# A GRU step on one core: the products of c ahead of those of r with one signal for both, and both vocabulary units of a block together, with one signal that also stands for the z products

## The reference

```python
x = emb_table[input_ids]                      # 2048 x 50 x 128
xp = einsum('bth,hk->btk', x, kernel) + b_i   # k = 3 * 128: z, r, h
def step(h, xt):
    rec = h @ rec_kernel + b_r
    xz, xr, xh = split(xt, 3);  rz, rr, rh = split(rec, 3)
    z = sigmoid(xz + rz)
    r = sigmoid(xr + rr)
    hh = tanh(xh + r * rh)
    h_new = z * h + (1 - z) * hh
logits = h_at_last_position @ emb_table.T     # 2048 x 12501, written out in float32
```

## Time and profile before

| | |
|---|---|
| median of 3 runs | 1207.63 us (1206.48 to 1207.8) |
| profiled execution: its own time | 1205.95 us |
| profiled execution: span from the first to the last instruction | 1204.1 us |
| TensorE busy, share of the span | 1064.9 us, 88% |
| VectorE busy | 798.4 us, 66% |
| ScalarE busy | 693.7 us, 58% |
| GpSimd busy | 763.7 us, 63% |
| mean granted TensorE clock, share of full speed | 0.989 |
| stage B, about | 91 to 591 us from the span's start |
| stage C, about | 591 to 974 us |
| stage D, about | 974 to 1124 us |
| tail, about | 1124 to 1204 us |

### The profile page before, as it was taken

How to read it: one execution, slowest core, us unless ns; L and a number is a source line. 1 busy time by engine, 2 the same in 40 slices (tenths; PEclk the granted TensorE clock), 3 DMA queues, 4 the chain that set the end, 5 groups by cost and what they waited for, 6 DMA issues and landing times.

```text
span 1204.1 us, 17546 instructions
## 1 busy us (share of the span) xinstructions
PE 1064.9 (88%) x6031; PEld 804.9 (67%) x6031; DVE 798.4 (66%) x1481; ACT 693.7 (58%) x1203; POOL 763.7 (63%) x812
## 2 busy tenths in 40 slices
PE   7968777877777778777899999999999999999997
PEld 6964444444444444444588888888888888888775
DVE  5745555555555555555677777888888887777644
ACT  4443444444444444444477777777777788888543
POOL 0017777777777777777777777777777777663000
PEclk9989999999999999999999999999999999999999
DMA  8986565656565656565588889989899999997799
GB/s 259 350 320 175 167 175 166 176 166 175 167 176 167 175 167 175 166 175 167 169 258 288 290 295 297 297 294 297 291 296 291 296 298 331 310 306 270 257 356 324
DMA packets 127495, 294.29 MB, mean 244 GB/s; under 512 B 18096, under 2 KB 33456, under 8 KB 127408
## 3 DMA queue, kind: packets, MB, share of 16 engines
q0 software_dynamic: 51200, 157.34, 45.3%
q1 hardware_dynamic: 76208, 135.84, 31.2%
HBM read 171.30 MB, written 121.81 MB: 243 GB/s over the span
## 4 chain that ended last, share of the span: by engine, by line
PE 56%; POOL 26%; issue 11%; DMA 5%; DVE 1%; ACT 0%; SPq 0%; DVEq 0%; ACTq 0%
POOL gathered L369 26%; PE x_ps L452 6%; PE x_ps L453 6%; PE x_ps L454 6%; PE r_ps L419 3%; DMA out_dram<-logits 3%; PE c_ps L419 3%; PE r_ps L432 3%; PE z_ps L432 3%; PE z_ps L419 3%; PE r_ps L433 2%; PE r_ps L436 2%; PE c_ps L432 2%; PE c_ps L433 2%; PE c_ps L436 2%
## 5 line engine op out<-in xcount | busy, mean ns | idle before, releaser
L369 POOL DMA_INDIRECT gathered<-gate_table,index x800 | 761.8, 952 | 338.1 <-issue 229.4
L570 ACT ACTIVATE table_rows<-r_ps,zr_bias 128x512 f32<-128x512 f32 (+1 forms) x250 | 151.2, 605 | 200.7 <-PE r_ps L427 162.6
L704 DVE SCALAR_TENSOR_TENSOR c_ps<-c_ps,bias_sb,table_rows 128x512 f32<-128x512 f32 (+1 forms) x250 | 162.8, 651 | 132.1 <-PE c_ps L427 98.6
L572 ACT ACTIVATE z_ps<-z_ps,zr_bias 128x512 f32<-128x512 f32 (+1 forms) x250 | 144.2, 577 | 182.4 <-PE z_ps L427 143.0
L562 ACT ACTIVATE logits<-x_ps,nan_row 128x512 f32<-128x512 f32 (+1 forms) x325 | 214.4, 678 | 42.8 <-PE x_ps L454 27.9
L709 DVE TENSOR_TENSOR table_rows<-z_ps,state 128x512 f32<-128x512 f32 (+1 forms) x250 | 145.0, 580 | 113.6 <-ACT z_ps L572 113.4
L419 PE MATMUL r_ps<-ident,gathered 128*128 128x128 f32 x800 | 107.6, 248 | 119.3 <-issue 107.6
L713 DVE SCALAR_TENSOR_TENSOR c_ps<-z_ps,table_rows 128x512 f32<-128x512 f32 (+1 forms) x250 | 147.7, 591 | 59.8 <-ACT table_rows L579 59.4
L419 PEld LDWEIGHTS r_ps<-ident,gathered 128*128 128x128 f32 x800 | 84.9, 141 | 138.2 <-issue 131.5
L716 DVE TENSOR_TENSOR state<-table_rows,c_ps 128x512 f32<-128x512 f32 (+1 forms) x250 | 145.3, 581 | 26.1
L579 ACT ACTIVATE table_rows<-c_ps,bias_sb 128x512 f32<-128x512 f32 (+1 forms) x250 | 149.7, 599 | 16.2 <-PE c_ps L419 14.7
(11 more groups left out here) (97 smaller groups left out, 1538.8 us busy)
## 6 DMA issues: line engine op xcount, KB each, us to landing
out_dram<-logits SPq DMA_DIRECT2D x192, 512.0 KB, 4.5
gate_table<-table_rows SPq DMA_DIRECT2D x24, 768.0 KB, 5.5
gathered<-gate_table,index POOLq DMA_INDIRECT x800
emb_rows<-in_L_rec_emb_table_dram SPq DMA_DIRECT2D x48, 256.0 KB, 5.8
out_dram<-logits SPq DMA_DIRECT2D x8, 213.0 KB, 3.7
logits<-in_r_input_ids_dram SPq DMA_DIRECT2D x1, 400.0 KB, 4.8
logits<-in_r_input_mask_dram SPq DMA_DIRECT2D x1, 400.0 KB, 6.2
gate_table<-table_rows SPq DMA_DIRECT2D x2, 192.0 KB, 9.3
```

The lines of the kernel that those rows point to most:

```text
L369: nc.gpsimd.indirect_dma_start(tile_rows(slot, n).bitcast(F32), None, table, bass.IndirectOffsetOnAxis(ap=index[:, tile, b.t:b.t + 1], axi ...
L570: nc.scalar.activation(r, r_bank, ACT.Sigmoid, bias=zr_bias[:, 1:2]).then_inc(s_r, 1)
L704: nc.vector.scalar_tensor_tensor(out=c_bank, in0=c_bank, scalar=bias_sb[:, 1, 2:3], in1=r, op0=ALU.add, op1=ALU.mult).then_inc(s_scaled, 1)
```

## The change

It does four things.

1. In `step`, the products of c are issued ahead of those of r, and only the last product of r raises `s_rec`, once for a block. Sigmoid r and the scaling on VectorE both wait for that one signal.
2. In a wide block both units stand ahead of the c rows, as they already do in a narrow block. The new `units` of `schedule` gives each block how many units stand in front of the c rows (2 in stages C and D, 0 in B) and behind them (always 0).
3. A unit's first bank no longer has its own signal: `s_unit` is raised once for a pair, with the last product of unit 1. Both copies wait for it, in the tail too.
4. In a block with units `s_z_in` is not raised. Sigmoid z waits for `s_unit` of the block's pair, which is raised later on the same engine than the z products. In stage B sigmoid z waits for `s_z_in` as before.

The place of the copies on ScalarE stays: ahead of tanh in a narrow block (`early`), behind it in a wide one.

```diff
 def schedule(T):
-    return order, 2 * T, lambda g: g >= 2 * T, [range(0, 4), range(4, 6), range(6, 8)]
+    def units(g):
+        if g < 2 * T:
+            return 0, 0, False
+        return (2, 0, False) if order[g][2] == LANE else (2, 0, True)
+
+    return order, 2 * T, units, [range(0, 4), range(4, 6), range(6, 8)]
...
 def unit(pair, j, bank):
-                nc.tensor.matmul(bank[:, 0:even], low, embT_hi[:, bass.ds(pair.v0, even)],
-                                 start=False, stop=True).then_inc(s_unit, 1)
+                last = nc.tensor.matmul(bank[:, 0:even], low, embT_hi[:, bass.ds(pair.v0, even)],
+                                        start=False, stop=True)
+                if j == UPP - 1:
+                    last.then_inc(s_unit, 1)
...
                 if not b.split:
+                    add_state(c_bank, h, 2, True)
                     add_state(r_bank, h, 1, False).then_inc(s_rec, 1)
-                    add_state(c_bank, h, 2, True).then_inc(s_rec, 1)
                     add_rows(z_bank, b, 0, True)
-                    add_state(z_bank, h, 0, False).then_inc(s_z_in, 1)
+                    z_done = add_state(z_bank, h, 0, False)
                 else:
                     pe.wait_ge(s_state_hi, blocks[b.prev].parts)
+                    add_high(c_bank, high, 2, True)
                     add_high(r_bank, high, 1, False)
-                    add_high(c_bank, high, 2, True)
                     pe.wait_ge(s_state_lo, blocks[b.prev].parts)
+                    add_low(c_bank, low, 2)
                     add_low(r_bank, low, 1).then_inc(s_rec, 1)
-                    add_low(c_bank, low, 2).then_inc(s_rec, 1)
                     add_rows(z_bank, b, 0, True)
                     add_high(z_bank, high, 0, False)
-                    add_low(z_bank, low, 0).then_inc(s_z_in, 1)
+                    z_done = add_low(z_bank, low, 0)
+                if not b.front:
+                    z_done.then_inc(s_z_in, 1)
                 if b.vocab >= 0:
                     vocabulary(b.vocab)
-                if b.pair >= 0:
-                    unit_beside(b.pair, 0)
-                    if b.width < LANE:
-                        unit_beside(b.pair, 1)
+                for w in b.front:
+                    unit_beside(w)
                 pe.wait_ge(s_scaled, g + 1)
                 add_rows(c_bank, b, 2, False).then_inc(s_turned, 1)
-                if b.pair >= 0 and b.width == LANE:
-                    unit_beside(b.pair, 1)
+                for w in b.behind:
+                    unit_beside(w)
...
 def copy_unit(u, j, bank):
-                act.wait_ge(s_unit, UPP * u + j + 1)
+                act.wait_ge(s_unit, u + 1)
...
 def gate(g, b):
-                act.wait_ge(s_rec, 2 * g + 1)
+                act.wait_ge(s_rec, g + 1)
                 nc.scalar.activation(r, r_bank, ACT.Sigmoid, bias=zr_bias[:, 1:2]).then_inc(s_r, 1)
-                act.wait_ge(s_z_in, g + 1)
+                if b.front:
+                    act.wait_ge(s_unit, b.front[-1] // UPP + 1)
+                else:
+                    act.wait_ge(s_z_in, b.alone)
                 nc.scalar.activation(z_bank, z_bank, ACT.Sigmoid, bias=zr_bias[:, 0:1]).then_inc(s_z, 1)
...
 def update(g, b):
-                dve.wait_ge(s_rec, 2 * g + 2)
+                dve.wait_ge(s_rec, g + 1)
```

More of the change, by code:

```diff
@@ L39 @@
     vocab: int = -1
-    pair: int = -1
+    front: range = range(0)
+    behind: range = range(0)
+    early: bool = False
+    alone: int = 0
 @dataclass
@@ L57, in schedule @@
     order = [lanes[0], lanes[1]] * T + [lanes[2], a, lanes[2], b] * (T // 2) + [a, b] * (T - T // 2)
-    return order, 2 * T, lambda g: g >= 2 * T, [range(0, 4), range(4, 6), range(6, 8)]
+    def units(g):
[3 more added lines that the diff above has]
+    return order, 2 * T, units, [range(0, 4), range(4, 6), range(6, 8)]
 def plan(T, chunks):
-    order, split_from, carries, groups = schedule(T)
+    order, split_from, units, groups = schedule(T)
     RING = 8
@@ L100, in plan @@
         blocks[4 * i].vocab = i
-    pairs, carriers = [], [g for g in range(len(blocks)) if carries(g)]
+    unit = 0
+    for g, b in enumerate(blocks):
+        front, behind, b.early = units(g)
+        b.front, b.behind = range(unit, unit + front), range(unit + front, unit + front + behind)
+        unit += front + behind
+        assert front in (0, 2) and behind == 0
+        b.alone = sum(not before.front for before in blocks[:g + 1])
+    assert unit % 2 == 0
+    pairs = []
     for group in groups:
@@ L106, in plan @@
             for h in group:
-                u = len(pairs)
-                pairs.append(Pair(2 * h, v0, width, blocks[latest[h]].parts if i == 0 else 0))
-                if u < len(carriers):
-                    assert latest[h] < carriers[u] and carriers[u] > 4 * len(chunks) - 4
-                    blocks[carriers[u]].pair = u
+                parts = blocks[latest[h]].parts if i == 0 else 0
+                for b in blocks:
+                    if 2 * len(pairs) in (*b.front, *b.behind):
+                        assert blocks.index(b) > max(latest[h], 4 * len(chunks) - 4)
+                pairs.append(Pair(2 * h, v0, width, parts))
     assert len(pairs) == 2 * LANES * len(chunks)
-    return blocks, pairs, len(carriers)
+    return blocks, pairs, unit // 2
 def gru_logits(nc, ids, mask, emb, w_in, w_rec, bias, out):
@@ L453, in unit, with unit_beside @@
                 nc.tensor.matmul(bank[:, 0:even], high, embT_lo[:, bass.ds(pair.v0, even)], start=False, stop=False)
-                nc.tensor.matmul(bank[:, 0:even], low, embT_hi[:, bass.ds(pair.v0, even)],
-                                 start=False, stop=True).then_inc(s_unit, 1)
-            def unit_beside(u, j):
+                last = nc.tensor.matmul(bank[:, 0:even], low, embT_hi[:, bass.ds(pair.v0, even)],
+                                        start=False, stop=True)
+                if j == UPP - 1:
+                    last.then_inc(s_unit, 1)
+            def unit_beside(w):
+                u, j = w // UPP, w % UPP
                 pair = pairs[u]
@@ L574, in gate @@
                     high_part(b.vocab)
-                if b.pair >= 0 and b.width < LANE:
-                    for j in range(UPP):
-                        copy_unit(b.pair, j, x_ps[:, j])
+                if b.early:
+                    for w in b.front:
+                        copy_unit(w // UPP, w % UPP, x_ps[:, w % UPP])
                 act.wait_ge(s_turned, g + 1)
                 nc.scalar.activation(new, c_bank, ACT.Tanh, bias=bias_sb[:, 0, 2:3]).then_inc(s_cand, 1)
-                if b.pair >= 0 and b.width == LANE:
-                    for j in range(UPP):
-                        copy_unit(b.pair, j, x_ps[:, j])
+                for w in (*(() if b.early else b.front), *b.behind):
+                    copy_unit(w // UPP, w % UPP, x_ps[:, w % UPP])
             for g, b in enumerate(blocks):
@@ L727, in _ @@
                 pair, p = pairs[u], u % PUTS
-                dve.wait_ge(s_unit, UPP * u + 2)
+                dve.wait_ge(s_unit, u + 1)
                 if u >= PUTS:
```

## The result

The changed kernel takes 1248.68 us (median of 4 runs, 1247.1 to 1251.04), the kernel before 1207.72 (4 runs): a ratio of 1.0337, 95% interval 1.0322 to 1.0351. It is 41 us slower. The forecast was 1256, in a range of 1236 to 1266.

The account below looks back on a forecast made before the run. It took gathers to bound B, TensorE C and D, and output writes the tail. D's 20.8 us plus C's 31 less 3 gave 49 us on the profiled execution's 1205.95, so 1255, forecast as 1256, range 1236 to 1266.

Parts of the forecast that it names:

- rival (1): Whole kernel: TensorE gets time back and nothing else moves, 1200 to 1205 us, middle 1203; chance 0.06.
- Sigmoid z behind the units: ScalarE's queue in C and D: later tanh and sigmoid r delay c rows, costing 31 us in C, 20.8 in D.
- The signal's cost: From the end of `scaled` to the c rows: distance TensorE needs, taken as 0.25 us.
- The upper bound of 0.27: Stage B: 0.27 us from the end of `scaled` through the c rows' extra length, read as the signal's cost.
- The prediction's other bound: Wide block of C: unhindered c rows leave room for only some 0.2 us of signal cost.
- The first pairs of C: Start of C: pairs waiting for late gathers, which a slower TensorE finds landed; 3 us taken off.
- Fewer signals: TensorE in C and D: 450 signals less, taken as 0 gain, bound 4.5 us.
- the spared switch: Wide blocks of C: one switch from transposes to products less, 0.06 us each; taken as 0, at best 3 us.
- c ahead of r: Sigmoid r's signal one product later: covered in C and D, taken as 0 in B.
- stage B on the path: Stage B: without the 3.97 us free, up to 1.09 us a round, 55 us more, 1311; chance 0.05.
- one stage alone: Only C stalls, 1236 us, or only D, 1229; chance 0.09 (0.05 and 0.04).
- no change: Whole kernel: sigmoid's delay absorbed and TensorE gains nothing, 1208 us; chance 0.03.

Follow-up runs that it names:

- f1: Kernel before with every second gather left out; 1087.02 us.
- e5: Kernel before, but in blocks with a pair sigmoid z waits for the pair's last unit; 1405.20 us amid stops, ratio 1.0055 to 1.0109.
- f3: Changed kernel with z's own signal back and every second gather left out; 1153.91 us.
- f2: Changed kernel with every second gather left out; 1176.50 us.
- f4: Kernel before with both units of a wide block ahead of the c rows and every second gather left out; 1099.43 us.
- e4: Kernel before with both units ahead of the c rows in wide blocks, all signals kept; 1389.37 us amid stops, ratio 0.9948 to 1.0006.
- e2: Changed kernel with z's own signal and one for each unit back; 1392.11 us amid stops, ratio to kernel before 0.997 to 1.002.
- e1: Changed kernel with z's own signal back in every block; 1397.38 us amid stops, ratio to kernel before 1.0002 to 1.0065.
- e8: Changed kernel with each unit's signal back, sigmoid z still waiting for the last; 1420.72 us amid stops, ratio to kernel before 1.0125 to 1.0244.
- e6: Kernel before with 800 more TensorE signals that nobody waits for; 1400.69 us amid stops, ratio 1.0012 to 1.0072.
- e7: Changed kernel with r ahead of c again and a signal each; 1410.83 us amid stops, ratio to kernel before 1.0058 to 1.017.
- e3: Kernel before with c's products ahead of r's and one signal for both; 1399.61 us amid stops, ratio 1.0008 to 1.0056.
- run 1223: Not a run's label: the count of matmuls executed in f4's 200 us window of stage C, against 1263 in f1.

## Why the prediction was right, and where it was off

**The bound of each stage** was read rightly: B at the gathers' pace (500.0 and 501.1 us; 389.1 with half the gathers, f1), C and D at TensorE's, with the wait for `scaled` as the place where a delay would come in. It left out that C has a second limit close by. GpSimd issues 80 gathers in the 100 us of C's window, as in B, and its median distance from one to the next is 1.25 us there; a pair has six, 7.5 us of its 7.59. By these numbers rival (1) could have gained no more than an estimated 4 us in C.

**Sigmoid z behind the units** makes the loss, by the chain forecast, but is not alone in it. In D e5 makes the 3.37 us with that wait alone. Undoing it gives only about half back: f3 lies 22.6 us below f2, which lost 43 in C and D. What stays is the units' place in the wide block (f4, 12.4 us; e4 and e2, 0.24 us a pair) and the first copy's wait for the pair (D 3.18 against 3.01, e1 and e2, 8.7 us over f1 in f3's D). The prediction had these two parts at 0, or inside the chain, and did not say what each would cost with z's own signal kept. In D the losses don't add up: sigmoid z's wait covers the first copy's (e8). In C no run has z's late wait alone with both units in front, so there only its share on top of the units' place is shown, 13.5 of 25.5 us.

**The signal's cost, 0.25 us, was the mis-sized term.** In the timeline of the changed kernel `scaled` ends at 1105.32, the c rows start at 1105.37 and take 0.37 us where unhindered ones take 0.29: 0.05 + 0.08 = 0.13. The upper bound of 0.27 came from stage B, where the c rows took 0.67 in place of 0.46 behind the signal. But there the float32 product for z ahead of them was still running, until 403.38 + 1.09 = 404.47, with the c rows from 404.11. The row of it in the kernel before:

```profile
403.38 1.09 PE L427 MATMUL z_ps<-state,w_rec_sb 128*128 128x512 f32 x2
```

In f1 it is the same picture, with the product until 302.99 and the c rows from 302.62, 0.67 long. In f2, where the product is over when the signal comes, they start 0.05 behind it and take 0.53: 0.05 + 0.07 = 0.12. So half of my 0.27 was a product's tail and no signal. The prediction's other bound, some 0.2 in the wide block of C, spoke against 0.25 already. With 0.13 the slack is 0.23 in a block of D and 0.45 in the narrow block of C, and the terms become 50 x (0.94 - 0.23) / 2 = 17.8 and 50 x (0.95 - 0.45) = 25 less 3: 39.8 us, against 38.6 measured in C and D. That the total of 41 us lies a little nearer to the 49 forecast is the tail's doing, and luck.

**The first pairs of C** lost less, as forecast: the first five pairs take 39.6 us in place of 39.4, 0.2 more where five steady ones lose 2.6. 2.4 us were hidden behind late gathers there, and 50 x 0.51 - 21.0 = 4.5 in all of C, since some later pairs wait for gathers too; I had taken off 3. With half the gathers, where none is late, C loses the whole 25.5 (f1 and f2).

**Fewer signals** gave nothing that shows (e6, where more signals left the spacing of products as it was), and neither did **the spared switch** between transposes and products (e4 and f4). **c ahead of r** cost nothing in the kernel as it is (B in the table of stages; C and D in e7), because of two covers: the gathers in B (worth 46 us, f1 and f2), and in C the units ahead of the wide block's c rows (e3 without them: 0.15 us a pair, by three pairs).

**The tail** took 2.6 us more, which I had at 0. In part it is TensorE's clock: the window after the last block of the changed kernel, and the next,

```profile
1166.00:1172.00 6.00, 5.53 (x20) 4.55 (x21) 2.10 (x5) 1.37 (x3) 0.00 (x0) 0.72 0.42 147
1172.00:1240.00 68.00, 65.74 (x275) 50.46 (x273) 34.57 (x47) 31.71 (x47) 0.00 (x0) 1.00 0.98 349
```

have a granted clock of 0.72 and 1.00; within the first, seven products of 512 columns stand 0.43 us apart and not 0.23, which is the 1.2 GHz level, after TensorE had waited 1.65 us for the last state. That is 7 x 0.20 = 1.4 us. The kernel before waits 1.6 us at that place and has no such products. Over all kernels the last block and tail take 81.8 to 85.9 us: 81.8 to 83.3 in the six that have no such slow products (before, e1, e4, e8, f1, f2), and the three longest, 85.2, 85.8 and 85.9, have ten, seven and eleven (f3, the changed kernel, e5). The order doesn't follow the edits, so I count this as scatter and not as an effect of the change.

**Rivals.** TensorE getting time back, stage B on the path, one stage alone and no change: all four fall by the table of stages. Stage B's did come true with half the gathers: 46 us, where it had up to 55.

## What to carry to other kernels

Before merging a signal into a later one, follow the queue of the engine that waits for it: what stands behind the waiting instruction is late too, and if that queue feeds back to the engine whose signals were saved, the delay less the slack is paid in every round. Measure the slack at the place where the loop closes (here from the end of `scaled` to the c rows), not from busy shares, and take the price of a signal from a place where nothing else is still running. An order that looks free may be hidden by a slower stream: take half of that stream away and look again.

## What the hardware showed that was not expected

A TensorE that the profile calls fully busy can still be waiting. In stage C of f1 and of f4, windows of 200 us:

```profile
560.00:760.00 200.00, 200.00 (x1263) 170.34 (x1262) 159.12 (x316) 151.04 (x263) 75.81 (x80) 1.00 0.66 217
```

```profile
560.00:760.00 200.00, 200.00 (x1223) 165.30 (x1222) 152.81 (x307) 139.25 (x257) 78.41 (x77) 1.00 0.62 211
```

Both are busy for 200.00 of 200 us, but the second has run 1223 matmuls and the first 1263. A matmul is shown 0.39 us long where the next starts after 0.23, so gaps of up to 0.16 us in the stream don't show. The count shows them: it is 3% less, as a pair of blocks is 3% longer (7.85 in place of 7.60).

The stops that brought the kernel before from 1208 to 1394 us came in the runs e1 to e8 and, for the kernel before, beside f1 to f4 too (1403 us), and were gone in f1 to f4 themselves, on the same chip, with half the gathers: f1's pair in C and block in D take what those of the kernel before take (7.60 and 3.01). So halving the gathers removed the stops, and the full stream alone does not bring them, since the kernel before ran in 1208 us with it. What stops the engines is open; no run here was made for it.

No version here beats the kernel before: e2, e3, e4 and e6 are equal to it in D and none is below it in C.
